# A two-network graph kernel on one core: byte scatters tied in fours to TensorE's pairs of attributes, sums in three PSUM banks, and the first gathers moved behind a barrier

## What is computed

```python
h = relu(layernorm(x));  x = x + L0(h, src, dst)
h = relu(layernorm(x));  x = x + L1(h, src, dst, edge_attr_64)
# L0, three times:
msg = relu(x[src]) + 1e-7
out = segment_softmax_sum(msg, dst) + x        # sum of msg * softmax(msg) over a node's edges
h   = relu(batchnorm(out @ W1 + b1));  x = relu(h @ W2 + b2)
# L1, three times (only the last node values are returned):
h = relu(x @ nw.T);  e = relu(ea @ ew.T)
n2 = relu(concat(segment_sum(e, dst), h) @ fnw.T + fnb)
ea = relu(concat(h[src] + h[dst], e) @ few.T + feb);  x = n2 * g / sqrt(1 + 1e-5) + b
```

## Time and profile before

| | us |
|---|---|
| median of three timed runs (4755.52 to 4767.22) | 4765.41 |
| the profiled execution's own time | 4728.06 |
| its span | 4726.3 |
| setup phase, to the first instruction behind its barrier | 1091 |
| three softmax layers with their node phases | 1091 to about 3228 |
| edge layers, from the first gathers | 3335 to the end |
| PE busy | 3580.1 (76%) |
| POOL busy | 2633.4 (56%) |
| DVE busy | 1855.2 (39%) |
| ACT busy | 1182.7 (25%) |

### The profile page before, as it was taken

The page is one execution under the profiler, slowest core; times in us unless marked ns, Lnnn a source line. Parts: engine busy times, 40 slices in busy tenths (PEclk is TensorE's granted clock), DMA queues, the critical chain, the costliest instruction groups (busy, mean ns, idle before and its releaser), DMA issues.

```text
span 4726.3 us, 73381 instructions
## 1 busy us (share of the span) xinstructions
PE 3580.1 (76%) x22631; PEld 2372.6 (50%) x22631; DVE 1855.2 (39%) x4048; ACT 1182.7 (25%) x2569; POOL 2633.4 (56%) x2750
## 2 busy tenths in 40 slices
PE   2111179996988978888887888988488888888888
PEld 1000046653555555455555555557366666666666
DVE  6000056541221337121227122218255555555555
ACT  1000033220000015000006000007244444544444
POOL 4777700004656656666664666665666666666663
PEclk6555589997999998899998999999799999999998
DMA  6000056555666646666655666665555555555553
GB/s 234 22 7 7 16 175 233 181 181 165 199 203 213 206 150 233 195 201 195 221 180 203 197 196 209 211 187 140 143 135 133 133 133 129 136 131 135 132 133 91
DMA packets 367696, 747.52 MB, mean 158 GB/s; under 512 B 102785, under 2 KB 197659, under 8 KB 366722
## 3 DMA queue, kind: packets, MB, share of 16 engines
q0 software_dynamic: 134912, 331.04, 24.7%
q1 hardware_dynamic: 224679, 362.01, 24.1%
q10 hardware_dynamic: 7899, 51.90, 2.8%
HBM read 613.65 MB, written 131.02 MB: 158 GB/s over the span
## 4 chain that ended last, share of the span: by engine, by line
PE 43%; another core or an unknown queue 19%; issue 18%; DVE 7%; SPq 6%; ACT 2%; DMA 1%; DVEq 1%; POOL 1%; ACTq 1%; POOLq 0%
PE ps L1486 17%; PE ps L1518 7%; PE ps L655 3%; PE ps L643 2%; PE ps L661 2%; SPq L2099 2%; PE ps L647 2%; PE ps L2151 1%; PE ps L2163 1%; SPq L2097 1%; PE ps L2132 1%; PE ps L1837 1%; PE ps L2169 1%; SPq L2096 1%
## 5 line engine op out<-in xcount | busy, mean ns | idle before, releaser
L601 POOL DMA_INDIRECT ring<-split_table,src_idx x1240 | 1181.6, 953 | 1188.5 <-PE ps L661 452.1
L1486 PE MATMUL ps<-spare,acc 128*128 128x500 fp8e4 x5292 | 1196.5, 381 | 185.1 <-issue 78.0
L2122 POOL DMA_INDIRECT ring<-h_table,idx_ring x832 | 837.9, 1007 | 494.0 <-remote 230.2
L1486 PEld LDWEIGHTS ps<-spare,acc 128*128 128x128 bf16 x5292 | 519.5, 99 | 801.8 <-issue 201.3
L1518 PE MATMUL ps<-ring,onehot 128*84 128x256 bf16 x3720 | 486.4, 286 | 90.4 <-issue 89.6
L1587 DVE TENSOR_TENSOR onehot<-onehot,ps 128x168 f32<-128x168 f32 x165 | 54.2, 328 | 1269.6 <-PE ps L1497 770.9
L612 POOL DMA_INDIRECT adjacency<-acc x408 | 416.7, 1021 | 180.6 <-issue 128.6
L1431 ACT ACTIVATE work<-ps 84x256 f32<-84x256 f32 x155 | 58.9, 380 | 1734.6 <-remote 1133.1
L1518 PEld LDWEIGHTS ps<-ring,onehot 128*84 128x84 bf16 x3720 | 426.1, 124 | 124.0 <-issue 118.2
L2132 PE MATMUL ps<-ident,ring 128*128 128x128 f32 x1664 | 271.6, 285 | 86.5 <-DMA acc<-e_few 55.8
L2169 PEld LDWEIGHTS ps<-mats,work 128*128 128x128 f32 x1664 | 235.4, 203 | 128.6 <-issue 128.0
(11 more groups left out here) (329 smaller groups left out, 4710.2 us busy)
## 6 DMA issues: line engine op xcount, KB each, us to landing
acc<-split_table SPq DMA_DIRECT2D x104, 768.0 KB
spare<-adjacency SPq DMA_DIRECT2D x108, 512.0 KB
e_few<-spare SPq DMA_DIRECT2D x104, 512.0 KB
acc<-e_few SPq DMA_DIRECT2D x208, 256.0 KB
work<-in_edge_attr SPq DMA_DIRECT2D x104, 256.0 KB
spare<-rel_rows SPq DMA_DIRECT2D x208, 126.0 KB
split_table<-acc ACTq DMA_DIRECT2D x32, 768.0 KB, 3.3
ring<-split_table,src_idx POOLq DMA_INDIRECT x1240
```

Of the source, the lines that this page charges most:

```text
L601: e.indirect_dma_start(out=to, out_offset=None, in_=table, in_offset=bass.IndirectOffsetOnAxis(ap=src_idx[:, 2 * i + h, j:j + 1], axis=0)) ...
L1486: ins = e.matmul(ps[2 + 2 * c + kind][:, 0:width], split[j % 2][:, k, q, kind * D:(kind + 1) * D], moving, start=(b == q == 0), stop=(b == ...
L2122: e.indirect_dma_start(out=rows[:, s, j, :], out_offset=None, in_=h_table, in_offset=bass.IndirectOffsetOnAxis(ap=idx_ring[:, s, j:j + 1], ...
```

## The change

Five edits.

1. `scatters`: each four of scatters also waits until PE has raised `few_e0` for `pairs_behind(n)` pairs: none for the fours 0 to 15, one pair for four 16, then nine pairs to every eight fours, up to 96 pairs for four 101.
2. The 24 gathers of the first three pairs leave the end of the setup phase; layer 0 now issues them itself, as the other layers do.
3. Softmax layers: a pair's sums are transposed, added and placed one step later (`late` 2 to 3), with PSUM banks 0, 1 and 7 taken in turn and a third `by_node` buffer. Three waits become a pair looser. At the end, `behind_sums` takes two pairs in step 55, so that the last pair is transposed in the same step as before. The jobs that follow a sparse chunk start a step later.
4. The column numbers of the one-hot matrices are read from `iota_w` in SBUF instead of PSUM bank 7, and DVE writes the next one-hot matrix ahead of the additions.
5. Edge layers: the comparison at L2256 becomes a `tensor_tensor` with a broadcast operand instead of a `tensor_scalar`.

```diff
@@ -93,7 +93,7 @@
 
 def dense_jobs():
 
-    jobs = [(pairs_of(c) + 3, c * CH, pairs_of(c), True) for c in range(CUT // CH)]
+    jobs = [(pairs_of(c) + 4, c * CH, pairs_of(c), True) for c in range(CUT // CH)]
     chunks = 0
     for r, (at, widths) in enumerate(REGIONS):
 for width in widths:
@@ -609,9 +609,15 @@
         n = i // EACH
         if i % EACH == 0 and n >= SCATTERS:
             e.wait_ge(S(f"gather_spread{n % SCATTERS}"), 16 * EACH * (n // SCATTERS))
+        if i % EACH == 0:
+            reached(e, S("few_e0"), 2 * pairs_behind(n))
         e.indirect_dma_start(out=adjacency, out_offset=bass.IndirectOffsetOnAxis(ap=spread_i[:, i:i + 1], axis=0),
                              in_=count_8[:, i:i + 1], in_offset=None
                              ).then_inc(S(f"gather_spread{n % SCATTERS}"), 16)
+
+def pairs_behind(n):
+
+    return min(NPAIR, max(0, 9 * n // 8 - 17))
 
 def scattered(e, S):
     for b in range(SCATTERS):
@@ -828,14 +834,8 @@
         if again:
             return
         scatters(e, S)
-        e.wait_ge(S("src"), 16)
-        e.wait_ge(S("rel_out"), 32)
+        scattered(e, S)
         split_stored0(e, S)
-        e.wait_ge(S("sums"), NPAIR)
-        e.wait_ge(S("few_e0"), 2 * NPAIR)
-        for i in range(SLOTS3):
-            pair_gathers(e, S, i, 0)
-        scattered(e, S)
 
     def dve(e, S):
         e.memset(Z0[:, HALF_Z:NP], 0.0).then_inc(S("half_zero"), 1)
@@ -1235,11 +1235,12 @@
     attr, term = layer == 0, layer == 1
     ready = layer == 0
     whole = 0 if ready else WHOLE
-    late = 2
+    late = 3
     sums = [flat_hot[:, SLOTS * 2 * J * WW + b * 4 * WW:SLOTS * 2 * J * WW + (b + 1) * 4 * WW].rearrange("p (k w) -> p k w", k=2)
             for b in range(SLOTS)]
-    columns = ps[7][:, 0:WW]
-    by_node = [work[0:WW, b, 0:2 * D] for b in range(2)]
+    columns = iota_w[:, :]
+    by_node = [work[0:WW, 0, 0:2 * D], work[0:WW, 1, 0:2 * D], work[0:WW, 0, 2 * D:4 * D]]
+    SUM_BANKS = [0, 1, 7]
 
     over_window = window_all[:, :, :].rearrange("p s c -> p (s c)").bitcast(F32)
     aggr = [over_window[:, GE + b * WW:GE + (b + 1) * WW] for b in range(3)]
@@ -1295,8 +1296,15 @@
     def tail_bank(n):
         return tail_banks[n - len(JOBS)]
 
+    def bank_of(k):
+        return ps[SUM_BANKS[k % 3]]
+
     def turned(k):
-        return ps[k % 2][:, 2 * D:2 * D + 2 * WW].rearrange("p (k w) -> p k w", k=2)
+        return bank_of(k)[:, 2 * D:2 * D + 2 * WW].rearrange("p (k w) -> p k w", k=2)
+
+    def behind_sums(i):
+
+        return {PAIRS: [PAIRS - 3, PAIRS - 2], PAIRS + 1: [PAIRS - 1], PAIRS + 2: []}.get(i, [i - late])
 
     def rows_landed(e, S, k):
         for h in range(2):
@@ -1358,7 +1366,7 @@
         e.wait_ge(S("params"), 16)
 
     def pool(e, S):
-        for i in range(SLOTS3 if layer == 0 else 0, PAIRS):
+        for i in range(PAIRS):
             reached(e, S("sums"), free_after(i, whole))
             if not ready and i == WHOLE:
                 for b in range(6):
@@ -1427,8 +1435,8 @@
             k = i - 1
             if whole <= k < PAIRS:
                 e.wait_ge(S("sums"), k + 1)
-                reached(e, S("turned"), k - whole - 1)
-                e.activation(by_node[k % 2], ps[k % 2][0:WW, 0:2 * D], ACT.Copy).then_inc(S("by_node"), 1)
+                reached(e, S("turned"), k - whole - 2)
+                e.activation(by_node[k % 3], bank_of(k)[0:WW, 0:2 * D], ACT.Copy).then_inc(S("by_node"), 1)
             for n, node, least, sparse in jobs_of(i - 1):
                 e.wait_ge(S("W1"), n + 1)
                 for h in range(2):
@@ -1490,19 +1498,19 @@
                 ins.then_inc(S("dense"), 1)
 
         for i in range(PAIRS + 3):
-            k = i - 2
-            if whole <= k < PAIRS:
-                e.wait_ge(S("by_node"), k - whole + 1)
-                for kind in range(2):
-                    ins = e.transpose(turned(k)[:, kind, :], by_node[k % 2][:, kind * D:(kind + 1) * D], ident[0:WW, 0:WW])
-                ins.then_inc(S("turned"), 1)
+            for k in behind_sums(i):
+                if whole <= k < PAIRS:
+                    e.wait_ge(S("by_node"), k - whole + 1)
+                    for kind in range(2):
+                        ins = e.transpose(turned(k)[:, kind, :], by_node[k % 3][:, kind * D:(kind + 1) * D], ident[0:WW, 0:WW])
+                    ins.then_inc(S("turned"), 1)
             if i == PAIRS:
                 W1_of_tail(e, S, TAIL[0])
                 W1_of_tail(e, S, TAIL[1])
             k = i - 1
             if 0 <= k < PAIRS:
                 b = slot_of(k)
-                reached(e, S("acc"), k - 1)
+                reached(e, S("acc"), k - 2)
                 e.wait_ge(S("onehot"), k + 1)
                 if k < whole:
                     e.wait_ge(S("mexp"), k + 1)
@@ -1515,7 +1523,7 @@
                         if t % J == 0:
                             half_landed(e, S, k, t // J)
                         for q in range(3):
-                            ins = e.matmul(ps[k % 2][0:WW, 0:2 * D], hot_b[k % SLOTS][:, t, :],
+                            ins = e.matmul(bank_of(k)[0:WW, 0:2 * D], hot_b[k % SLOTS][:, t, :],
                                            pair_parts[b][:, t, q * 2 * D:(q + 1) * 2 * D], start=(t == q == 0),
                                            stop=(t == 2 * J - 1 and q == 2))
                 ins.then_inc(S("sums"), 1)
@@ -1538,7 +1546,6 @@
         for t in sums:
             e.memset(t[:, 0, :], TINY).then_inc(S("zero"), 1)
             e.memset(t[:, 1, :], 0.0).then_inc(S("zero"), 1)
-        e.tensor_copy(columns, iota_w[:, :]).then_inc(S("zero"), 1)
 
         def times_rows(u):
             n = blocks_of(u)
@@ -1570,7 +1577,7 @@
             times_rows(0)
             for u in range(2):
                 unit(u)
-        e.wait_ge(S("zero"), 2 * SLOTS + 1)
+        e.wait_ge(S("zero"), 2 * SLOTS)
 
         def onehot_of(i):
             reached(e, S("sums"), i - SLOTS + 1)
@@ -1637,15 +1644,13 @@
                 m = pair_rows[:, b, :, 0:D]
                 e.scalar_tensor_tensor(out=m, in0=m, scalar=EPS_MSG, in1=pair_rows[:, b, :, D:2 * D], op0=ALU.add,
                                        op1=ALU.mult).then_inc(S("mexp"), 1)
-            k = i - late
-            placing = 0 <= k < PAIRS
-            if placing:
-                add_up(k)
             if i + 1 < PAIRS:
                 onehot_of(i + 1)
-            if placing:
-                divide(k)
-                place(k)
+            for k in behind_sums(i):
+                if 0 <= k < PAIRS:
+                    add_up(k)
+                    divide(k)
+                    place(k)
             for c in range(2):
                 for r in evacuated(i - c):
                     quotients(r, c)
@@ -2253,7 +2258,7 @@
         def hots(i):
             wait(e, S(f"rel{i.off % 4}"), i, 4, 16 - 4 * (i.off % 4))
             wait(e, S("turn2"), i - 4)
-            e.tensor_scalar(onehotT[:, i.off % 4, :], relb[:, i.off % 4, :], iota_p[0:3 * W, :], None,
+            e.tensor_tensor(onehotT[:, i.off % 4, :], relb[:, i.off % 4, :], iota_p[0:3 * W, :].broadcast_to([3 * W, GE]),
                             ALU.is_equal).then_inc(S("one_hotT"), 1)
 
         def step(i):
```

## The result

The changed kernel takes 4460.51 us (median of four, 4457.13 to 4467.23) against 4764.57 for the kernel before: ratio 0.9367, interval 0.9349 to 0.9385. A second measurement, in a later job, gave 4434.55 against 4759.43: 0.930 (0.9269 to 0.9331). The forecast was 4400, with 4345 to 4460 as its own range and 4295 to 4560 as the whole one. The first measurement stands at the upper edge of the forecast's own range, the second inside it.

A forecast was written before the change was run, and what follows sets the result against it. Setup was held to be bound by POOL's unbroken scatters slowing instruction issue on several engines. Terms -377 + 13 - 10 + 10 = -364 on the profiled 4728 gave 4364, plus 37 to the median: 4400; range 4295 to 4560.

The forecast's parts named there:

- the store: Setup: something fills as POOL gives one DMA per 1.26 us and passes one per 1.40; source of the delay not shown.
- Edit 1, first pairs at 165: Setup with tied scatters: PE's pairs start at 165 us, 30 us earlier than before.
- Edit 1, 5.2 us a pair: Tied part of the setup: a pair takes 5.2 us, against 4.98 without loss; 96 pairs take 499 us.
- half a gain: Rival, tied part: idle PE and a falling clock make pairs 6.8 us, +154 us, 4555 us in all; chance 0.19.
- Edit 2, +13: Layer 0: issuing 24 first gathers there costs PE +10 us, and +3 for the first dense loads (0 to +25).
- The crawl: Layer 0: 24 gathers without a pause slow PE to about an instruction per 1.4 us, taken as +10 us.
- Edit 3, -10: Softmax layers: the later step removes idle time ahead of the transpose (L1497), -12 to 0 us, taken as -10.
- Edit 4, hidden: Layers, L490: at most 908 ns, up to +0.1 us on DVE 165 times, hidden; POOL's gathers up to 0.9 us more.
- Edit 5, +10: Edge layers, L2256: +0.34 us x 208 = 71 us of DVE time, partly hidden; taken as +10 us.
- The fixed toll: Rival, setup: every scatter holds other engines 1.40 us whenever issued; 9.29 us a pair, 4794 us; chance 0.07.
- no crawl: Rival, tied part: PE never crawls, a pair costs POOL's 4.48 us, 69 us less, 4332 us; chance 0.15.
- only in the profiled run: Rival, setup: the stall exists only in the profiled execution, so the stage stays; 4748 us; chance 0.03, shared with not POOL's doing.

## Why the prediction was right, and by how much it was off

- **What bounds the kernel.** Right: without scatters PE runs free. That it takes an unbroken row above a rate is right too: nearly free at 1.54 us, held at 1.32, and the held pitch is 1.40 to 1.41 whether POOL tries for 1.26 or 1.32. The row need not be long, though: I read rows of eight as free, from layer 0, where PE is idle 1.0 us beside one; in the tied part they cost 2.4 us each. What the store is I had left open; it is not made of unlanded scatters, and the limit shows on some chips and not on another, with one and the same kernel. POOL's issuing is not the whole cause, since the faster chip takes it at 1.26 us without loss.
- **Edit 1, first pairs at 165.** They start at 157.
- **Edit 1, 5.2 us a pair.** This is the term that was mis-sized: 5.8 us. The 95 pairs took 551 us where I had 499 for 96: +52, less 4 at the start of the tied part and 10 behind it, where 35 us were left to the barrier's end and not 45. The setup ends at 752, not 714. I took the loss as 0.2 us over the saturated pitch. What the trace has over the free pair of 4.31 us is 1.5 us: in the 564 us PE is idle for 86, and its 2930 matmuls take 478 us where at the pace of rows 2 (424 for 2934) they would take 423, with the granted clock at 0.93 and not 0.99. So something of the rival "half a gain" came true, idle time and with it a lower clock: 5.8 us lie 0.6 above my term and 1.0 below that rival's 6.8.
- **Edit 2, +13.** Layer 0 grew by 16 us, edits 3 and 4 included; in the seven slower-chip profiles with the gathers in the layer it takes 721 to 733 us, 716 before. The crawl was forecast on PE; the trace has PE's first dense block 13.7 us behind the barrier, 10.2 before.
- **Edit 3, -10.** It brought nothing. Some of the waits for ACT did go, which the profile before, with few of them, hides: on PE alone they are 14, 7.5 and 14 us in the three slower-chip profiles with the edit and 12 to 37 in the six without. But PE's idle time ahead of the next matmuls, the sums (L1526, L1518 before), is 117 to 137 us with the edit and 44 to 90 without, nearly all of it "issue". I had put the looser order at no cost there. Edits 3 and 4 together cost some 20 us in layer 1, and no slower-chip run separates them: 751, 734 and 745 us in the three profiles with them, 718 to 728 in the six without.
- **Edit 4, hidden.** L490 takes 849 ns, under the bound of 908. Hidden on DVE, as said, but not on POOL: my estimate ("up to 0.9 us more and still fit") had the right mechanism and called it harmless. The mean gather went from 953 to 981 ns; on the faster chip, where POOL bounds the layers, the operand alone adds 22 us to them.
- **Edit 5, +10.** The profile shows +26, but 20 or more of it is the short edge stage of the profile before. Against six other profiles with the old form (1411 to 1422) the changed kernel's 1417 and 1414 are no cost that shows. This comparison too has two SBUF inputs now, and the edge layers' gathers go from a mean of 1007 ns to 1029, for which POOL, idle 502 us before them, has room.
- **The sum.** Profiled: 4364 + 38 (setup) + 58 (behind it: +71 measured, +13 forecast) = 4460, the profiled 4460.15. The 37 us that I added from profile to median were real for the kernel before, and most of them probably lay in its edge layers (1391 against 1411 to 1422); the profile of the changed kernel had none to add. So the forecast is 38 + 58 - 37 = 59 us too low by the profile, 60.5 by the median, and would have been 96 too low without these 37: that part of the agreement is luck.
- **The fixed toll** is refuted by the spacing of 1.54 us, **no crawl** by the trace (PE idle 86 of 564 us), **only in the profiled run** by the timed runs without scatters. By the rule on taken branches (Trainium skill, Runtime: NRT & Kernel Launch, Instruction fetch mechanics) the stalls would be the loop's; the same loop ran without any when the scatters were left out, so the trace doesn't bear it out here.

## What to carry to other kernels

When all engines slow to the same beat while POOL issues indirect DMAs, change the pitch before the structure: a dummy POOL instruction behind each DMA shows at once whether a rate or a price per DMA is at work, and on the slower chips it was also the better cure (0.9196 against 0.930). Tying POOL to PE in fours works, but in bursts of eight and more that still cross the limit. And run the kernel before on more than one chip: the gain of 6 to 7% exists only on chips where the crawl does; on the other one the tie (measured with edit 2 and the columns, not as the whole change) is worth nothing measurable and the spacing costs 2%.

## What was not expected of the hardware

- Two chips run one kernel in 4760 us and a third in 3713 us. The kernel with 8 in flight, which ran on both kinds, has the same POOL queue packets on them and nearly the same packet time (1153 and 1146 us). The difference is in stretches with indirect DMAs: from the last gather of a layer to the first of the next stage there are 251 us in all on the slower chip and 234 on the faster.
- On the slower chips the engines' instructions come 1.4 us apart when POOL's scatters come at 1.26 or 1.32 us in long unbroken rows, and not at 1.54 us, and a limit on scatters in flight does not change it. Where the limit sits stays open.
- A gather on POOL takes 1.50 us and not 0.95 when it begins just behind a DVE instruction of 0.85 us with two SBUF inputs; with one operand in PSUM it does not grow (none of some 70 over 0.96 us).
